# The rotary part of a two-layer attention kernel moved from GpSimd to VectorE and ScalarE

## The reference

```python
def _layer(x, wqkv, qs, ksc, wo, lg, lb, w1, b1, w2, b2):
    qkv = shift_token(x) @ wqkv
    q, k, v = jnp.split(qkv, 3, axis=-1)          # 8 heads of 64
    q = l2norm(q) * qs
    k = l2norm(k) * ksc
    q, k = rotary_xpos(q, k)      # q*cos*scale + rotate_half(q)*sin*scale
    o = local_attention(q, k, v)  # windows of 128, each sees itself and the one before
    x = x + o @ wo
    ...
```

## Time and profile before

| | |
|---|---|
| median of 3 runs | 2297.49 us (2285.77 to 2298.86) |
| the profiled execution, its own time | 2309.4 us |
| its span, first to last instruction | 2307.6 us |
| mean granted TensorE clock | 0.951 |

### The profile page before, as it was taken

One profiled execution on the slowest core, in us unless ns is written; L12 is line 12 of the kernel. 1 busy time (PEld: TensorE's weight loads), 2 busy tenths in 40 slices (PEclk: granted clock), 3 DMA queues, 4 the chain that ended last, 5 costly groups with the idle time before them and its releaser, 6 DMA issues.

```text
span 2307.6 us, 29326 instructions
## 1 busy us (share of the span) xinstructions
PE 2057.9 (89%) x8706; PEld 1222.2 (53%) x8707; DVE 1090.2 (47%) x3036; ACT 899.8 (39%) x2175; POOL 682.6 (30%) x664
## 2 busy tenths in 40 slices
PE   4773999995799999998999999989999998999897
PEld 2531666663465555555555555555555555555552
DVE  5543222221555555454555546454555554564541
ACT  0010333332345445452535344434545353544442
POOL 5065000002632343242323425132353432232310
PEclk9965999997899999999989999999999999999999
DMA  8332212122100010010000102000010100000000
GB/s 254 109 116 97 64 61 60 59 61 66 19 19 1 1 28 1 28 28 29 1 1 1 28 1 55 19 11 1 1 28 1 42 14 19 1 1 1 1 19 9
DMA packets 71773, 78.21 MB, mean 34 GB/s; under 512 B 17156, under 2 KB 63704, under 8 KB 71640
## 3 DMA queue, kind: packets, MB, share of 16 engines
q1 hardware_dynamic: 56104, 58.68, 8.1%
q0 software_dynamic: 12672, 17.87, 3.8%
q10 hardware_dynamic: 2864, 0.01, 0.1%
HBM read 48.19 MB, written 28.35 MB: 33 GB/s over the span
## 4 chain that ended last, share of the span: by engine, by line
PE 47%; issue 10%; DVE 9%; ACT 6%; POOL 4%; DMA 1%; ACTq 0%; DVEq 0%; POOLq 0%
PE pj L1340 10%; PE pj L1253 9%; PE pj L1346 6%; PE ob L1300 5%; PE pj L1314 4%; DVE swapped L1523 3%; PE sc L1276 3%; PE pt L1287 3%; PE pj L1261 2%; ACT prob L1404 2%; POOL x1tok L1470 2%; PE pj L1327 1%; DVE direct L1518 1%; PE pj L1243 1%; PE pj L1321 1%
## 5 line engine op out<-in xcount | busy, mean ns | idle before, releaser
L1481 POOL TENSOR_TENSOR qksq<-qkraw 128x512 f32<-128x512 f32 x128 | 162.8, 1298 | 856.1 <-ACT qkraw L1381 856.1
L1253 PE MATMUL pj<-wqkv,xT 128*128 128x512 f32 x768 | 349.0, 604 | 10.2 <-issue 10.2
L1340 PE MATMUL pj<-h,w 128*128 128x512 f32 (+1 forms) x704 | 341.2, 610 | 10.4 <-DVE h L1570 6.1
L1404 ACT ACTIVATE prob<-prob,nm 128x256 f32<-128x256 f32 (+1 forms) x512 | 240.0, 470 | 218.2 <-DVE nm L1542 217.8
L1300 PEld LDWEIGHTS ob<-vv,pT 128*128 128x128 f32 x1792 | 231.5, 199 | 86.4 <-issue 70.1
L1300 PE MATMUL ob<-vv,pT 128*128 128x64 f32 x1792 | 233.9, 278 | 32.3 <-DVE pT L1174 32.3
L1523 DVE TENSOR_TENSOR swapped<-qkraw,tabs 128x256 f32<-128x256 f32 x256 | 252.4, 1024 | 0.0
L1253 PEld LDWEIGHTS pj<-wqkv,xT 128*128 128x128 f32 x768 | 144.4, 193 | 192.0 <-issue 185.6
L1487 POOL TENSOR_TENSOR direct<-direct,swapped 128x512 f32<-128x512 f32 x128 | 187.5, 1480 | 72.3 <-DVE swapped L1523 72.3
L1518 DVE TENSOR_TENSOR direct<-qkraw,tabs 128x512 f32<-128x512 f32 x128 | 103.3, 807 | 205.2 <-ACT qkraw L1381 205.2
L1340 PEld LDWEIGHTS pj<-h,w 128*128 128x128 f32 (+1 forms) x704 | 120.6, 189 | 129.2 <-issue 118.4
(11 more groups left out here) (246 smaller groups left out, 2633.8 us busy)
## 6 DMA issues: line engine op xcount, KB each, us to landing
xt<-slots_x SPq DMA_DIRECT2D x72, 128.5 KB, 2.1
slots_y<-yt SPq DMA_DIRECT2D x72, 128.0 KB, 1.7
xin<-in_x_dram SPq DMA_DIRECT2D x8, 512.0 KB
w1m<-in_L_ffn_w_dram SPq DMA_DIRECT2D x8, 512.0 KB
w2m<-in_L_ffn_w_dram SPq DMA_DIRECT2D x8, 512.0 KB
x1tok<-in_x_dram SPq DMA_DIRECT2D x8, 512.0 KB, 4.6
x_after_moe<-x1tok SPq DMA_DIRECT2D x8, 512.0 KB, 2.6
x1out<-x_after_moe SPq DMA_DIRECT2D x8, 512.0 KB, 4.6
```

Source lines behind the costliest of these rows:

```text
L1253: mm = pe.matmul(o[:, :], xs(s, c, w * P, P), wqkv[:, l, c, k * INNER:(k + 1) * INNER], start=(c == 0), stop=(c == DC - 1))
L1340: mm = pe.matmul(o[0:P if j == NJ - 1 else HJ[j], :], cols, h[:, c, :], start=(c == 0), stop=(c == DC - 1))
L1404: ins = a.activation(prob[:, g % 4, hh, 0:n], prob[:, g % 4, hh, 0:n], ACT.Exp, bias=nm[:, g % 4, hh:hh + 1], scale=-1.0, accum_out=rs[:, ...
L1481: pool.tensor_tensor(qksq[:, k * INNER:(k + 1) * INNER], src, src, ALU.mult).then_inc(squared, 1)
```

## The change

GpSimd has no part in `qkv`, `rope` and `norm` any more, only its `pick` steps. The squares are one ScalarE instruction of 1024 columns that stands behind the copy of v. On VectorE the six products of `rope` become three on q and k together (1024, 512 and 512 columns), and behind them, still in the step `rope`, stand the sum of squares, the addition of the products (1024 columns) and the floor. In `norm` VectorE waits for `rn` and makes the product `roped` (1024 columns). TensorE's `turn` waits once instead of twice.

```diff
                         elif kind == "turn":
+                            pe.wait_ge(rope_done, at(st["win"], i, WIN, 1, 1))
                             for k in range(2):
                                 o = bank(u + k, i)
-                                pe.wait_ge(rope_done, at(st["win"], i, WIN, 2, k + 1))
...
                         elif kind == "qkv":
...
                                 a.copy(dst, o[:, :]).then_inc(proj_taken[(u + k) % NP], 1)
+
+                            wait(a, summed, at(st["win"], i, WIN))
+                            for k in range(2):
+                                wait_taken(a, u + k, i)
+                            a.activation(qksq[:, :], raw[:, st["win"] % 2, :, :].rearrange("p k n -> p (k n)"), ACT.Square
+                                         ).then_inc(squared, 1)
...
-                        if kind == "qkv":
-                            for k in range(2):
-                                wait_taken(pool, st["use"] + k, i)
-                                if k == 0:
-
-                                    wait(pool, summed, at(st["win"], i, WIN))
-                                src = raw[:, st["win"] % 2, k, :]
-                                pool.tensor_tensor(qksq[:, k * INNER:(k + 1) * INNER], src, src, ALU.mult
-                                                   ).then_inc(squared, 1)
-                        elif kind == "rope":
-                            for k in range(2):
-                                n = 2 * st["win"] + k
-                                pool.wait_ge(parts_ready, at(n, i, 2 * WIN, 1, 1))
-                                pool.tensor_tensor(direct[:, k, :], direct[:, k, :], swapped[:, k, :], ALU.add
-                                                   ).then_inc(added, 1)
...
                         if kind == "rope":
...
-                            wait(v, rope_done, at(win, i, WIN, 2))
+                            wait(v, rope_done, at(win, i, WIN))
                             for k in range(2):
                                 wait_taken(v, st["qkv_use"] - 2 + k, i)
...
+                            src = raw[:, win % 2, :, :].rearrange("p k (h d) -> p k h d", h=H)
+                            t = tabs[:, l, 0:4:2, w, :].unsqueeze(2).to_broadcast([P, 2, H, DH])
+                            v.tensor_tensor(direct[:, :, :].rearrange("p k (h d) -> p k h d", h=H), src, t, ALU.mult)
+                            sw = swapped[:, :, :].rearrange("p k (h d) -> p k h d", h=H)
+                            for half in range(2):
+                                d0, s0 = half * DH // 2, (1 - half) * DH // 2
+                                t = tabs[:, l, 1:4:2, w, d0:d0 + DH // 2].unsqueeze(2).to_broadcast([P, 2, H, DH // 2])
+                                ins = v.tensor_tensor(sw[:, :, :, d0:d0 + DH // 2], src[:, :, :, s0:s0 + DH // 2], t,
+                                                      ALU.mult)
+                            ins.then_inc(parts_ready, 1)
+                            v.wait_ge(squared, at(win, i, WIN, 1, 1))
+                            v.tensor_reduce(ss[:, :], qksq[:, :].rearrange("p (h d) -> p h d", h=2 * H), AX.X, ALU.add
+                                            ).then_inc(summed, 1)
+                            v.wait_ge(parts_ready, at(win, i, WIN, 1, 1))
+                            v.tensor_tensor(direct[:, :, :], direct[:, :, :], swapped[:, :, :], ALU.add).then_inc(added, 1)
+                            v.wait_ge(summed, at(win, i, WIN, 1, 1))
+                            v.tensor_scalar(ss[:, :], ss[:, :], NORM_FLOOR, None, ALU.max).then_inc(floored, 1)
                         elif kind == "norm":
                             win = st["win"]
...
+                            v.wait_ge(added, at(win, i, WIN, 1, 1))
+                            v.wait_ge(norm_ready, at(win, i, WIN, 1, 1))
+                            v.tensor_tensor(
+                                roped[:, :, :].rearrange("p k (h d) -> p (k h) d", h=H),
+                                direct[:, :, :].rearrange("p k (h d) -> p (k h) d", h=H),
+                                rn[:, :].unsqueeze(2).to_broadcast([P, 2 * H, DH]), ALU.mult).then_inc(rope_done, 1)
```

More of the change, by code:

```diff
@@ L1372, in one @@
                         elif kind == "qkv":
-                            wait(a, parts_ready, at(st["win"], i, WIN, 2, -2))
+                            wait(a, parts_ready, at(st["win"], i, WIN, 1, -1))
                             for k in range(3):
@@ L1473, in one @@
                                     compute_op=ALU.add).then_inc(picked[k], 16)
-                        if kind == "qkv":
-                            for k in range(2):
-                                wait_taken(pool, st["use"] + k, i)
-                                if k == 0:
-                                    wait(pool, summed, at(st["win"], i, WIN))
-                                src = raw[:, st["win"] % 2, k, :]
-                                pool.tensor_tensor(qksq[:, k * INNER:(k + 1) * INNER], src, src, ALU.mult
-                                                   ).then_inc(squared, 1)
-                        elif kind == "rope":
-                            for k in range(2):
-                                n = 2 * st["win"] + k
-                                pool.wait_ge(parts_ready, at(n, i, 2 * WIN, 1, 1))
-                                pool.tensor_tensor(direct[:, k, :], direct[:, k, :], swapped[:, k, :], ALU.add
-                                                   ).then_inc(added, 1)
-                        elif kind == "norm":
-                            for k in range(2):
-                                n = 2 * st["win"] + k
-                                pool.wait_ge(added, at(n, i, 2 * WIN, 1, 1))
-                                if k == 0:
-                                    pool.wait_ge(norm_ready, at(st["win"], i, WIN, 1, 1))
-                                pool.tensor_tensor(
-                                    roped[:, k, :].rearrange("p (h d) -> p h d", h=H),
-                                    direct[:, k, :].rearrange("p (h d) -> p h d", h=H),
-                                    rn[:, k * H:(k + 1) * H].unsqueeze(2).to_broadcast([P, H, DH]), ALU.mult
-                                ).then_inc(rope_done, 1)
                     walk(pool, one)
@@ L1531, in one @@
-                            v.wait_ge(summed, at(win, i, WIN, 1, 1))
-                            v.tensor_scalar(ss[:, :], ss[:, :], NORM_FLOOR, None, ALU.max).then_inc(floored, 1)
+                            v.wait_ge(added, at(win, i, WIN, 1, 1))
[4 more added lines that the diff above has]
+                                rn[:, :].unsqueeze(2).to_broadcast([P, 2 * H, DH]), ALU.mult).then_inc(rope_done, 1)
```

13 lines of the change are left out of this document (removed).

## The result

The changed kernel takes **2361.27 us** (median of 4 runs, 2346.67 to 2371.90) against 2294.49 for the kernel before (4 runs, 2285.77 to 2298.86): a ratio of 1.029, 95% interval 1.022 to 1.036, so 67 us slower. Timed once more, beside new runs of the kernel before, the ratio was 1.026 (1.023 to 1.030), which is 55 us. 2360 us was forecast, in a range of 2315 to 2390. The profiled execution took 2355.34 us, with a span of 2353.5 and a mean granted clock of 0.936 (before: 2309.4, 2307.6 and 0.951).

A forecast was written before the change was run, and what follows sets the result against it. TensorE was taken to set the pace, other engines counting only through its waits and clock. 30 us of waits plus 35 us of clock on the 2297.5 us median gave 2362, say 2360, range 2315 to 2390.

The forecast's parts named there:

- the 23 windows of the three kinds: The 15 fourth windows of the groups (3, 7, ... 59), five with a gelu between, and 14, 30, 46: longer TensorE waits.
- VectorE's instructions: With GpSimd silent, 1024 columns on VectorE take 1.22 us and hold it 1.14; 512 columns hold it 0.61.
- the clean rows: Profile rows without GpSimd slowing VectorE: 512 columns 691 ns, sum of squares over 1024 columns 1.20 us.
- the high bound of 5.4: If GpSimd doesn't cause the slow rows, the three products hold VectorE 5.4 us instead of 2.4.
- Windows without cover: Fourth windows, only attention on TensorE: copy to pT 1.55 later, mask 1.37; 16.4 us for 12, 2.1 for 11, 27, 43.
- Gelu windows: Windows 6, 22, 38, 54, 58: ScalarE's squares push back the gelu, first mask 1.9 later; 9.5 us in all.
- Windows 14, 30, 46: VectorE starts behind a value product; the last value product, for which TensorE waits, ends 0.94 later: 2.8 us.
- Picks: Where GpSimd's pick steps held it up, TensorE waited for roped; 3.8 us taken off.
- The clock: Idle times grown to 2 us or more bring 1.2 GHz stretches: 18 new ones, taken at 17 x 2.04 = 35 us.
- The clock didn't hold: Rival: the waits grow but the clock holds, 2327 us; chance 0.22.
- hidden cover: Rival: the chain's length is covered more than read, so nothing measurable, 2285 to 2318 us; chance 0.10.
- the worst case: Rival: three products cost what six did, windows of all kinds lose cover; over 2390 us, 2430; chance 0.05.

The follow-up runs named there:

- experiment 4: Changed kernel with the squares moved back from ScalarE to GpSimd (two of 512 columns), all else as changed: 2380.56 us, 1.031 of the kernel before.
- Experiment 3: Changed kernel with three useless 512-column matmuls filling TensorE's idle time before the first pv of each fourth window: 2351.99 us, 1.019 of the kernel before.
- squares_scalar: Kernel before with only the squares moved from GpSimd to one ScalarE instruction behind the copy of v: 2263.03 us, 0.980 of the kernel before.

## Why the prediction was right

The mechanism held: the places, the waits and the lower clock behind them are those of the forecast. That the time was met within 2 us is luck. The repeat of the measurement gave a loss of 55 us and not 67, where 65 had been put, and errors of the sum cancel. TensorE idled 20.5 us more and was busy 42 us more, where 30 and 35 had been put. By place, the 23 windows of the three kinds grew by 52.6 us where 31 for waits and 35 for the clock had been put, windows 0, 1, 2, 61 and 62 by 8.8 where 2.9 had been put, and the 35 others by 1.3 where 3.8 had been taken off.

- **VectorE's instructions.** 1.22 us was taken for 1024 columns from the clean rows and 1.22 measured. With GpSimd's squares beside them the three products would have taken 3.5 us and not 2.6 (experiment 4); the high bound of 5.4 was not reached even there.
- **Windows without cover.** Copy to pT at 5.90 forecast, 5.73 measured; idle time 3.0 forecast, 2.76 measured; mask 7.12 and 6.98. The pure cost, in window 39 and in the filled windows, is 1.25 us a window where 1.37 was put: 15.0 us for the 12. In 11, 27 and 43 the idle time grew by 0.50, not 0.7.
- **Gelu windows.** The mask was put 1.9 later and came 1.8 later; TensorE's idle time was put at 2.4 and was 2.27. 9 us of waits, 9.5 forecast. The second profile shows what they cost without the clock: its windows 38 and 54 have no slow stretch and took 31.4 us against 29.6 before, 1.8 more. Windows 14, 30, 46: 0.85 each (2.07 us of idle time against 1.23), 0.94 forecast.
- **Picks.** 3.8 us was taken off for the wait for roped. The wait, which lay in windows 16, 32 and 48 only, is gone, but the six windows in which picks lie (16, 18, 32, 34, 48, 50) got only 1.0 us shorter together. In window 16 TensorE idled 0.69 and 0.34 us for roped before, and 0.59 and 0.75 us for two of ScalarE's results (`oT` and `xsq`) in the changed kernel. This step failed, by 3 us.
- **The clock.** 17 new slow stretches were forecast. Counted behind the waits in question there were 5 of 15 and 0 of 8 before, and 14 of 15 and 8 of 8 after: 17 new. In the second profile it is 14 of 15 and 6 of 8, so 15. Counted everywhere from window 0 to the end, the rise is smaller, from 18 to 30, since some stretches of the kernel before, most of them in windows 19, 35 and 61, are missing after; together they lasted 96.8 us before and 195.6 after. In the fourth windows that have a clean partner one costs 1.5 to 2.9 us. TensorE's idle time in the windows rose from 104.6 to 125.1 us, 20.5 and not 30, because slow matmuls after a first wait eat up part of the next one: the wait for the exponentials behind it is 0.76 us in window 39, which kept its clock, and nothing in 35 (0.84 in both before), and all waits of that kind fell from 16.3 to 5.4 us. The remaining 42 us are matmuls at 1.2 GHz, where 35 had been put. Experiment 3 takes 23 to 25 us of the loss away in the fourth windows, with the value matmul as late as before. It leaves 35 us: the waits, and the eight stretches that weren't filled.
- **The range.** Its upper bound doesn't come out of the sum named beside it: 30 us of waits and 23 drops of 2.9 us give 2394 and not 2390. Nothing hangs on that.
- **Rivals.** The clock didn't hold, and the windows had no hidden cover. Windows 4, 5, 8, 9, 10, 12, 13 and 17 stayed the same to 0.01 us, and 37 too, so the worst case didn't come either. Of 36 and its like, 52, 56 and 60 got 2.3 us longer and 36 itself 1.5 shorter: no new wait, but a slow stretch that reaches over from the window before or no longer does, and in the second profile of the changed kernel 52, 56 and 60 are as before.

Open: what decides whether a given idle time is followed by 1.2 GHz. It isn't the window as such: at the same idle time of 2.76 us window 39 alone kept its clock in one profile of the changed kernel and window 31 alone in the other, where 38 and 54 kept it too. It isn't the length alone either: the wait of 2.9 us early in windows 19, 35 and 51, the same in every kernel, was followed by 1.2 GHz in 23 of 33 cases over the eleven profiles. Nor is it shown why three of the twelve windows with 1.44 us lost it in the kernel before.

## What to carry to other kernels

When TensorE is the bound, cost an edit to another engine by place: look up what stands in its queue ahead of each piece that TensorE waits for, in the windows without cover, and add a clock term, read from the trace's own slow stretches, for each idle time that grows. Busy time saved elsewhere is worth nothing by itself: here 472 us less of GpSimd work came with 67 us more. Try each part of a many-part change alone: the squares on ScalarE alone were worth 2%, so the rest of the change, which was not run by itself, took more than twice that back (from 0.980 to 1.026).

## What the runs showed of the hardware

- In the changed kernel idle times of 2.07 to 2.33 us (the gelu and the 14, 30, 46 kind) were followed by a stretch at 1.2 GHz in 8 of 8 windows of one profile and 6 of 8 of the other, and those of 2.76 to 2.82 in the fourth windows in 14 of 15 of each; in the kernel before, those of 2.26 in 2 of 3 and those of 1.44 to 1.49 in 3 of 12; those of 1.44 in the gelu windows of squares_scalar in 0 of 5. The same 2.76 us filled with matmuls without use: 0 of 15.
- Taking one GpSimd partner away (128 squares of 512 columns) took the mean of a 256-column product from 1024 to 564 ns, with the GpSimd additions (1406 ns) still beside them. VectorE got 118 us back there (252.4 to 134.1) and lost 8 in the products with the cosines (103.3 to 111.4), ScalarE paid 68 us for the squares.
- 1024 columns on VectorE are one instruction of 1.22 us; two of 512 are 1.28 back to back. Joining q and k saved next to nothing; it was GpSimd's silence that made them quick.
- The part ahead of window 0, the same in all these kernels but for its last microseconds, took 576 us in one profile and 588 to 594 in the other ten. A comparison of two single profiled executions can be off by 15 us from that alone.
